# Audio tower kernel: another order of the steps on all five engines, and eight PSUM tiles in other banks

## What is computed

```python
h = tok_ref(x)                      # z = tanh(conv), f, o = sigmoid(conv), kernel of 2 rows
                                    # c = f * c + (1 - f) * z, row by row;  h = o * c
h = h + attn_ref(layernorm(h))      # 8 heads of 16; each row looks at 39 rows back:
                                    # 0..32 and 48, 64, 96, 128, 192, 256, with a bias each;
                                    # softmax over the 39, times sigmoid(gate), out projection
h = h + ffn_ref(layernorm(h))       # 64 experts, top 2, at most 128 rows an expert (in row order);
                                    # one shared FFN 128 -> 512 -> 128 with gelu, weighted by the gates
```

## Time and profile before

| | |
|---|---|
| median of 3 runs | 430.35 us (429.63 to 431.35) |
| span of the profiled execution | 428.5 us |
| PE busy | 405.3 us, 95% |
| VectorE busy | 380.8 us, 89% |
| GpSimd busy | 372.7 us, 87% |
| ScalarE busy | 323.1 us, 75%, 40 table loads among it |
| DMA | 56.08 MB, mean 131 GB/s |

### The profile page before, as it was taken

The page is one execution under the profiler, slowest core; times in us unless marked ns, Lnnn a source line. Parts: engine busy times, 40 slices in busy tenths (PEclk is TensorE's granted clock), DMA queues, the critical chain, the costliest instruction groups (busy, mean ns, idle before and its releaser), DMA issues.

```text
span 428.5 us, 12683 instructions
## 1 busy us (share of the span) xinstructions
PE 405.3 (95%) x4554; PEld 278.6 (65%) x4554; DVE 380.8 (89%) x873; ACT 323.1 (75%) x728; POOL 372.7 (87%) x391
## 2 busy tenths in 40 slices
PE   8788789999999999999999999999999999998884
PEld 5444364776757676776767677676767675766763
DVE  2586999899999999999999999999999999999563
ACT  3756768879687877968687887868788796859773
POOL 7696999999989989898998989898998999997611
PEclk9999999999999999999999999999999999999998
DMA  6530866462737265372826446273735547265500
GB/s 230 192 105 2 200 165 182 105 174 62 200 88 183 79 154 150 86 207 61 198 71 149 143 120 186 55 201 82 178 95 129 158 109 190 65 182 127 133 13 24
DMA packets 78702, 56.08 MB, mean 131 GB/s; under 512 B 28304, under 2 KB 71344, under 8 KB 78512
## 3 DMA queue, kind: packets, MB, share of 16 engines
q1 hardware_dynamic: 78640, 55.28, 48.1%
HBM read 35.56 MB, written 19.70 MB: 129 GB/s over the span
## 4 chain that ended last, share of the span: by engine, by line
PE 74%; POOL 8%; issue 3%; DVE 3%; DMA 2%; ACT 1%; SPq 0%; POOLq 0%; DVEq 0%; ACTq 0%
PE bank L456 18%; PE bank L552 9%; PE bank L529 8%; PE bank L432 6%; PE bank L405 5%; PE bank L489 5%; PE bank L406 5%; PE bank L477 4%; POOL prod L1724 4%; POOL fprod L1709 3%; PE bank L468 3%; PE bank L521 2%; PE bank L505 2%; PE bank L440 2%; PE bank L424 1%
## 5 line engine op out<-in xcount | busy, mean ns | idle before, releaser
L1724 POOL TENSOR_TENSOR prod<-q,k 128x1448 f32<-128x1448 f32 (+2 forms) x48 | 145.6, 3053 | 17.4 <-ACT k L865 13.0
L1247 DVE SCALAR_TENSOR_TENSOR prod<-bank,par,k 128x1432 f32<-128x1432 f32 (+4 forms) x80 | 134.9, 1693 | 0.0
L456 PE MATMUL bank<-prod,ew 128*32 128x374 f32 (+7 forms) x1024 | 84.3, 467 | 2.4 <-ACT gate L872 1.0
L1709 POOL TENSOR_TENSOR fprod<-q,k 128x326 f32<-128x326 f32 (+6 forms) x112 | 79.0, 742 | 0.0
L456 PEld LDWEIGHTS bank<-prod,ew 128*32 128x32 f32 x1024 | 31.4, 110 | 44.9 <-issue 37.9
L972 ACT ACTIVATE hid<-bank,par 128x374 f32<-128x374 f32 x64 | 36.3, 575 | 23.8 <-PE bank L529 22.0
L799 ACT ACT_TABLE_LOAD x40 | 51.3, 1283 | 1.4 <-PEq L1944 0.7
L529 PE MATMUL bank<-x,par 128*128 128x374 f32 x128 | 48.4, 484 | 2.0 <-ACT x L925 2.0
L552 PE MATMUL bank<-par,hid 128*128 128x128 f32 x384 | 47.9, 276 | 0.0
L552 PEld LDWEIGHTS bank<-par,hid 128*128 128x128 f32 x384 | 45.9, 192 | 2.5
L405 PE MATMUL bank<-xT,par 128*128 128x374 f32 x96 | 40.9, 508 | 1.2 <-DVE mixin L1200 0.6
(11 more groups left out here) (123 smaller groups left out, 873.6 us busy)
## 6 DMA issues: line engine op xcount, KB each, us to landing
band<-band_scratch SPq DMA_DIRECT2D x16, 768.0 KB, 5.5
band_scratch<-attn SPq DMA_DIRECT2D x64, 180.4 KB, 3.0
vnear<-v_scratch SPq DMA_DIRECT2D x48, 192.0 KB, 3.1
v<-v_scratch SPq DMA_DIRECT2D x32, 192.0 KB, 4.1
v_scratch<-vtok SPq DMA_DIRECT2D x16, 192.0 KB, 3.0
xT<-x_dram SPq DMA_DIRECT2D x16, 187.5 KB, 3.4
vfar<-v_scratch SPq DMA_DIRECT2D x16, 128.0 KB, 3.3
out_dram<-osb SPq DMA_DIRECT2D x16, 128.0 KB
```

The costliest lines, as they stand in the source:

```text
L456: done = mm(home(f"s{c}")[32 * g:32 * g + 32, lo:N], ew[:, COLS[c] + j, :], src[:, j, lo:N], start=first or only, stop=last or only)
L1247: v.scalar_tensor_tensor(bass.AP(prod[c][:, :, :].tensor, first * N + lo, [[CW * N, 128], [N, w], [1, N - lo]]), home("q")[:, lo:N].unsque ...
L1709: last = g.tensor_tensor(fprod[:, i, o:N], q[q_.s][:, o:N], k[q_.s][:, KPAD:KPAD + N - o], ALU.mult)
L1724: g.tensor_tensor(bass.AP(prod[c][:, :, :].tensor, first * N + lo, [[CW * N, 128], [N, w], [1, N - lo]]), q[q_.s][:, lo:N].unsqueeze(1).br ...
```

## The change

All five lists are written in another order, for the first sequences, in the turns and for the last sequences. The steps are the same, with the same instructions; there are still 40 table loads. GpSimd's turn covers only its first four rounds now, and the rest of its list is written out. A turn begins at another place of the cycle on PE, ScalarE and VectorE. Eight entries of `HOME` change (k, tb1, tb2, x2b and the four up), and the names in front of PE's steps with them.

```diff
-        HOME = dict(z=4, f=1, o=7, ht=2, xb=0, q=3, k=7, v=1, g=5, ...
-                    tb1=0, tb2=6, pv=1, ot=1, op=0, x2b=4, lg=6, pos=7, up0=0, up1=5, up2=7, up3=4, dn=6)
+        HOME = dict(z=4, f=1, o=7, ht=2, xb=0, q=3, k=0, v=1, g=5, ...
+                    tb1=7, tb2=4, pv=1, ot=1, op=0, x2b=0, lg=6, pos=7, up0=4, up1=7, up2=5, up3=0, dn=6)
...
             def turn(at):                                 # SP
-                a0, a3, a4, a6 = at(0), at(3), at(4), at(6)
+                a1, a4, a5, a6, a10 = at(1), at(4), at(5), at(6), at(10)
+                if a6:
+                    write_attn(a6)
+                    read_band(a6)
+                if a5:
+                    read_near(a5)
+                    read_far(a5)
+                if a6:
+                    read_values(a6)
+                if a10:
+                    store_out(a10)
+                if a1:
+                    load_x(a1)
                 if a4:
-                    read_far(a4)
-                if a0 and not (isinstance(a0.b, int) and a0.b < 3):
-                    load_x(a0)
-                if a4:
-                    write_attn(a4)
-                    read_values(a4)
-                    read_band(a4)
-                if a3:
-                    write_values(a3)
-                    read_near(a3)
-                if a6:
-                    store_out(a6)
+                    write_values(a4)
...
             pipeline(sp, turn, range(5, 17))
+            write_attn(seq[11])
+            store_out(seq[7])
+            read_values(seq[11])
+            read_near(seq[12])
+            read_band(seq[11])
+            write_attn(seq[12])
+            read_far(seq[12])
+            write_values(seq[13])
+            store_out(seq[8])
...
```

More of the change, by code:

```diff
@@ L365, in _ @@
+            read_far(seq[12])
+            write_values(seq[13])
+            store_out(seq[8])
+            read_near(seq[13])
+            read_values(seq[12])
+            read_band(seq[12])
+            write_attn(seq[13])
+            write_values(seq[14])
+            read_values(seq[13])
+            read_band(seq[13])
+            store_out(seq[9])
             read_far(seq[13])
[L366 to L369, removed]
+            read_far(seq[14])
@@ L370, in _ @@
+            store_out(seq[10])
             read_near(seq[14])
-            read_far(seq[14])
             write_attn(seq[14])
+            write_values(seq[15])
+            read_band(seq[14])
+            read_near(seq[15])
             read_values(seq[14])
-            read_band(seq[14])
-            write_values(seq[15])
-            read_near(seq[15])
+            read_values(seq[15])
+            write_attn(seq[15])
             read_far(seq[15])
             store_out(seq[11])
-            write_attn(seq[15])
@@ L609, in turn @@
[L609 to L619, removed]
+                    project(a3, "k", ("xb", a3), head=True)
@@ new lines, in _ @@
+            turn_o(seq[12], ("pv", seq[12]))
+            up(seq[11], 0, ("tb2", seq[12]))
+            up(seq[11], 2, ("ts2", seq[13]))
+            up(seq[11], 1, ("tb1", seq[12]))
+            value_project(seq[14], ("ot", seq[12]))
+            out_project(seq[12], ("up3", seq[11]))
+            project(seq[14], "g", ("up2", seq[11]))
+            score(seq[14], 0, 1, ("up0", seq[11]), first=True)
+            down(seq[11], 0, ("lg", seq[11]), head=True)
+            positions(seq[11], ("up1", seq[11]))
@@ L1082, in _ @@
+            half_forget(seq[4])
+            norm1_rows(seq[2])
+            tanh_o(seq[3])
+            score_copy(seq[1], 1)
+            norm1_back(seq[2])
+            score_copy(seq[1], 0)
+            open_gate(seq[0])
+            score_copy(seq[1], 2)
+            open_gate(seq[1])
+            band_copy(seq[0], 0)
+            copy_k(seq[2])
             pipeline(act, turn, range(5, 17))
-            score_copy(seq[13], 2)
-            norm1_back(seq[14])
-            open_gate(seq[13])
```

906 lines of the change are left out of this document (518 added, 388 removed).

## The result

The changed kernel takes 483.0 us (median of 4 runs, 481.47 to 487.49) against 430.85 us for the kernel before (4 runs), a ratio of 1.1245 with a 95% interval of 1.1187 to 1.1304. Its profiled execution has a span of 482.2 us, 53.7 more than before. The forecast was 447, with a range of 431 to 455: slower, as forecast, but the loss is over three times as large.

A forecast was written before the change was run, and what follows sets the result against it. It took PE to bound the regular turns at 24.54 us. From the profiled span, 428.5 - 2.5 (first turns) + 18.9 (seven store waits) + 0.5 (regular turns) + 0 (last turns) = 445.4, plus 1.85 to the median: 447 us, range 431 to 455.

The forecast's parts named there:

- Step 3: On SP, write_values, four band writes and their landing before read_band can leave: 6.63 us after value_project began.
- Step 4: From read_band's issue to the store's landing, queued behind band, near, far and v: 9.9 us, bounds 8.9 and 12.1.
- Step 5: From finish through additions, maximum, subtraction and exponentials to PE's up 3: 6.0 us with the hops between engines.
- the rest of the regular turns: Regular turns apart from the store loop, with the eight moved PSUM homes: +0.5 us, 0 to 1.1 in eleven turns.
- the last turns: Last sequences: band read no longer behind v, sequence 15's attend behind an up and logits; 0, -1.9 to +1.3 us.
- Steps 1 and 2: PE from up 3 to value_project, 4.72 us; then through ScalarE's copy to SP's write_values, 1.39 us.
- the first rival: The store lands in time, 2.3 us after its issue; no turn grows, kernel faster at 428.3 us; chance 0.12.
- The first turns' -2.5: Sequence 1's k and q projections ahead of the fprod scores spare GpSimd's wait for copy_k: -2.5 us, -3.5 to +0.5.
- the 463 of step 4's own upper bound: Rival that something else is late too: 4.9 us in seven turns, 463 us; over 455 had chance 0.06.
- The partly hidden case: The store slips in between the reads, a turn grows by 0.3 to 1.7 us: 430 to 438 us, chance 0.12.

The follow-up runs named there:

- run 2: Changed kernel with SP's store of the same sequence issued ahead of the two reads of v instead of behind them; 462.8 us.
- run 7: Changed kernel with six more matmuls, read by nothing, on PE in the seven turns while it waits for the projection of q; 473.87 us.
- run 10: run 4 with project k and q of sequence 1 put back behind the fprod scores of sequence 0 on PE; 433.18 us.
- run 1: Changed kernel with SP's store of each sequence issued one turn earlier, at the same place of the turn; 445.77 us.
- run 6: run 4 with each band read ahead of the other reads in the last turns, and the load of x ahead of the store; 430.09 us.
- run 9: run 6 with write_attn ahead of the next write_values, except in the first of these turns: changed kernel, SP's list alone rewritten; 426.51 us.
- run 5: Changed kernel with finish on VectorE behind two of the three score_add instead of ahead of all; 469.41 us.
- run 4: Changed kernel with the store one turn earlier and the reads of v right behind the band's read, ahead of near and far; 430.32 us.
- run 8: Changed kernel with write_attn of a sequence ahead of write_values of the next, the store still last; 430.14 us.

## Why the prediction was right, and where it wasn't

**The direction and the mechanism** held. The loop from `value_project` over `write_attn`, the reads and the store to `finish` and back is what lengthens the turns, in the seven turns named, and `finish` of 9 and 10 find their stores landed. The size did not hold: 31.06 us a turn instead of 27.25. Steps 3, 4 and 5 of the loop were too short, and two terms beside it, the rest of the regular turns and the last turns, were put at next to nothing.

**Steps 1 and 2** came out to the hundredth: 4.73 (4.72) and 1.38 us (1.39).

**Step 3**, `value_project` to the issue of `read_band`, is 7.23 us on the mean of seven turns instead of 6.63: the four writes take 2.25 to issue, not 2.02, and land 2.5 to 3.9 us later, not 2.80. In the earlier trace rows no write of values stood ahead of them.

**Step 4**, from there to the landing, is 11.37 us instead of 9.9 and within its bounds of 8.9 to 12.1. SP's own issuing, up to the end of the store's, took 7.1 us on the mean (6.6 to 8.2) instead of the 4.7 that I counted at the small issues' price; but run 2 shows that the landing follows the issue only in part, and what the rest of it waits for stays open. The sum has a small slip too: the KB of the rows are of 1024 bytes, so 1275 KB take 3.84 us at 340 GB/s, not 3.75. The 2.3 us of the first rival is not what the store took in either place: on the mean 6.4 us from the start of its first issue in the changed kernel, 6.3 in run 2.

**Step 5**, `finish` to `up` 3, is 7.73 us instead of 6.0. Its path was wrong for this order: it left out that `project` q needs the bank of the first `score_add`, and that ScalarE's exponentials stand behind `copy_q`. That its length was nearly right all the same, 6.27 us with PE kept busy, is luck. What failed in its size is that it took PE's speed as given. PE stands still for some 5 us in such a turn and comes back at a lower clock, 1.46 us a turn by the difference to run 7, 10 us in all. The Trainium skill, page TensorE: Matmul & The Clock Gate, Part 1, says that an idle engine falls back to 1.2 GHz; the granted clock of 0.66 agrees.

Together, of the 26.8 us by which the seven turns were missed, 14.5 lie between `value_project` and `finish` (2.07 a turn), 10.2 are the clock, and the rest is the path of step 5.

**The first turns' -2.5** was right as a mechanism (run 10) and a little small (3.87 us at GpSimd's second run, of which 0.87 is an earlier start: `value_project` of 0 at 22.91 instead of 23.78). It didn't reach the end, because the reads of v at the end of SP's burst made `attend` wait 2.60 and 1.70 us. I had called `attend` "even to 0.1" by ScalarE's copies and looked at the store alone as the one that comes late in the burst; `read_values` stands right ahead of it and was late too, in the turns without a store as well (+2.31 instead of +0.5).

**The last turns' 0** failed by 5.74 us, most of it, 4.16, in the turn from 12 to 13. The profile after shows it: `turn_band` waits for a band that SP reads behind v and near.

```profile
367.21 0.44 SPq L283 DMA_DIRECT2D band<-band_scratch  x1
...
373.35 0.63 PE L484 MATMUL bank<-par,band 128*128 128x128 f32 x4 [2.66 <-DMA band<-band_scratch]
```

That order was in the list which I had read; I had priced only the one band that comes earlier. Behind this stand PE's clock was 0.73 up to 376.00 and 0.76 from there to 380.00, so the clock takes its part here too. With the store a turn earlier, and so out of the way of this read, 68.57 us are left in run 1; runs 6 and 9 have the bands first as well and take 67.28 us.

**The range** ended at 455, below the 463 of step 4's own upper bound. Even all the upper bounds on record added up (430.35 + 34 + 0.5 + 1.1 + 1.3) come to 467 only: steps 3 and 5 had no bounds of their own, the clock had no term at all, and v and the bands of the last turns were not among what can be late. All of them lay on the same side. The partly hidden case was cut short as well: 1.7 us in seven turns reach 440, not 438.

## What to carry to other kernels

When an order is changed, walk each loop that closes within a turn, and put bounds on all of its terms, not on the least known one; ask too of every transfer in a lengthened burst, not only of the last, who waits for it. A wait costs by what stands behind it: moving `finish` behind what others wait for won 24 us of the 483, the store a turn earlier 37, and the burst started earlier 53. A loop that makes PE stand still for microseconds can cost its clock on top.

## What the runs showed of the hardware

- PE's granted clock was 0.66 in the 5 us that followed a stand of 4.78 us, and stayed at 1.00 with matmuls in the gap; such stands cost 1.46 us a turn on the mean. Behind shorter ones it went both ways: 0.72 behind 2.15, 3.19 and 3.47 us (run 5), 0.73 behind 2.66 us, but 1.00 behind 2.37 and 2.89 us (run 5) and behind 2.60 us (at 58.17 in the changed kernel).
- An issue on SP isn't a fixed price: the first part of the same store took 0.47 us ahead of two reads of v and 1.23 to 2.82 behind them. In the changed kernel near, v and far land 5.0, 6.3 and 5.7 us after their issue:

```profile
vnear<-v_scratch SPq DMA_DIRECT2D x48, 192.0 KB, 5.0
v<-v_scratch SPq DMA_DIRECT2D x32, 192.0 KB, 6.3
...
vfar<-v_scratch SPq DMA_DIRECT2D x16, 128.0 KB, 5.7
```

- The four writes of the band, behind a write of values, were through 2.5 to 4.0 us after their last issue: for sequences 3 to 9 3.81, 3.14, 2.56, 3.82, 3.26, 2.62, 3.88 in the changed kernel and 3.89, 2.98, 2.52, 3.96, 3.39, 2.61, 3.93 in run 4, at other times and with other neighbours. It is not the same in every kernel: in run 7 sequences 6 and 7 take 2.79 and 2.57, and in runs 8 and 9, where these writes stand ahead of the write of values, all seven take 2.4 to 2.6 us. The cause is open.
- In runs 4, 6 and 10 PE stood still for 1.6 to 2.1 us, four times in all, with no releaser that the profile names, and each stand began 0.4 to 0.9 us after the fetch of a packet of code had, at the end of a burst of reads. But 36 or 37 such packets are fetched in each kernel here, and nearly all pass without a stand. That the fetch is the cause is argued from these four places, not shown.
